# Routed experts computed only for the tokens that chose them, by scatter through device memory

## The reference, cut to what matters

```python
scores = sigmoid(x @ gate_w.T)                 # [2048, 16]
topk_w, topk_ids = top_k(scores, 4); topk_w /= topk_w.sum(-1)
comb[t, topk_ids[t]] = topk_w[t]               # zero for the other 12 experts
eo = (silu(x @ Wg[e]) * (x @ Wu[e])) @ Wd[e]   # for every e
out = (silu(x @ sg) * (x @ su)) @ sd + sum_e comb[:, e] * eo[e]
```

## Time and profile before

| | us |
|---|---|
| median of three runs | 1480.97 |
| profiled execution, own time | 1483.09 |
| its span (first to last instruction) | 1481.7 |
| first matmul of `experts(0)` (L923) | 1141.10 |
| last group of matmuls of `experts(1)` (L940) begins | 1475.68 |

### The profile page before, as it was taken

One profiled execution on the slowest core, in us unless ns is written; L12 is line 12 of the kernel. 1 busy time (PEld: TensorE's weight loads), 2 busy tenths in 40 slices (PEclk: granted clock), 3 DMA queues, 4 the chain that ended last, 5 costly groups with the idle time before them and its releaser, 6 DMA issues.

```text
span 1481.7 us, 19507 instructions
## 1 busy us (share of the span) xinstructions
PE 1232.3 (83%) x7048; PEld 748.6 (51%) x7048; DVE 889.1 (60%) x2091; ACT 599.9 (40%) x1205; POOL 327.0 (22%) x327
## 2 busy tenths in 40 slices
PE   4568868976479934699999899898978999999998
PEld 2234645653336621243335333265544778777777
DVE  3676638575938575767675776177787575542322
ACT  2232146322255621356554465644435343232222
POOL 3410023220443220600000200033321232222222
PEclk9789998985889975799999999999997999999999
DMA  6144530360024300133322020060000000000000
GB/s 180 64 90 93 79 49 1 72 87 1 0 75 86 44 0 0 61 68 44 44 44 44 1 44 2 1 182 1 0 1 1 1 1 15 1 15 1 15 1 15
DMA packets 45919, 56.44 MB, mean 38 GB/s; under 512 B 8742, under 2 KB 30592, under 8 KB 45824
## 3 DMA queue, kind: packets, MB, share of 16 engines
q1 hardware_dynamic: 45824, 55.20, 18.6%
HBM read 40.37 MB, written 14.68 MB: 37 GB/s over the span
## 4 chain that ended last, share of the span: by engine, by line
PE 62%; DVE 22%; ACT 7%; issue 5%; POOL 2%; DMA 2%; SPq 0%; DVEq 0%; ACTq 0%; POOLq 0%
PE psum L923 12%; PE psum L940 7%; PE psum L814 5%; PE psum L602 5%; PE psum L784 4%; PE psum L833 4%; PE psum L684 3%; DVE mx L1639 3%; PE psum L709 2%; PE psum L695 2%; PE psum L503 2%; DVE stats L1254 2%; DVE small L1419 1%; PE psum L584 1%; PE psum L927 1%
## 5 line engine op out<-in xcount | busy, mean ns | idle before, releaser
L1639 DVE TENSOR_REDUCE mx<-psum 128x1 f32<-128x512 f32 (+3 forms) x384 | 200.1, 552 | 87.4 <-PE psum L787 63.1
L1865 POOL TENSOR_TENSOR work<-work,small 128x308 f32<-128x308 f32 x128 | 90.9, 713 | 312.6 <-DVE small L1435 312.6
L923 PE MATMUL psum<-H_r,area_r 128*128 128x512 f32 x408 | 145.6, 398 | 0.0
L1927 POOL TENSOR_TENSOR work_r<-work,work_r 128x512 fp32r<-128x512 f32 x68 | 89.3, 1313 | 250.1 <-ACT work_r L1214 250.1
L784 PE MATMUL psum<-stack_area 96*128 96x512 bf16 (+3 forms) x288 | 100.3, 353 | 45.9 <-DVE mx L1639 44.5
L1766 DVE TENSOR_TENSOR work<-work,psum 128x512 f32<-128x512 f32 x68 | 46.7, 687 | 150.3 <-PE psum L923 148.2
L1155 ACT ACTIVATE work<-psum 128x512 f32<-128x512 f32 (+1 forms) x192 | 94.7, 526 | 78.5 <-PE psum L836 59.9
L684 PE MATMUL psum<-area 128*128 128x308 f32 x256 | 100.7, 479 | 20.1 <-DVE work L1432 15.8
L1214 ACT CAST work_r<-work 128x512 fp32r<-128x512 f32 x68 | 42.2, 620 | 164.3 <-DVE work L1770 157.9
L1155 ACT ACTIVATE HT<-psum 128x384 f32<-128x384 f32 (+2 forms) x192 | 82.4, 454 | 47.6 <-PE psum L836 31.5
L833 PE MATMUL psum<-stack_area 98*128 98x512 bf16 (+3 forms) x288 | 94.9, 336 | 7.1 <-ACT work L1155 3.6
(11 more groups left out here) (254 smaller groups left out, 2721.5 us busy)
## 6 DMA issues: line engine op xcount, KB each, us to landing
stack_area<-parts_a0q SPq DMA_DIRECT2D x24, 128.0 KB, 4.2
stack_area<-parts_a0k SPq DMA_DIRECT2D x24, 128.0 KB, 7.0
stack_area<-parts_a1q SPq DMA_DIRECT2D x24, 128.0 KB, 4.6
stack_area<-parts_a1k SPq DMA_DIRECT2D x24, 128.0 KB, 7.2
stack_area<-parts_d0q SPq DMA_DIRECT2D x18, 128.0 KB, 4.3
stack_area<-parts_d0k SPq DMA_DIRECT2D x18, 128.0 KB, 7.1
stack_area<-parts_d1q SPq DMA_DIRECT2D x18, 128.0 KB, 4.1
stack_area<-parts_d1k SPq DMA_DIRECT2D x18, 128.0 KB, 6.7
```

The lines of the kernel that those rows point to most:

```text
L923: done = pe.matmul(u.bank(x), w[:, c, :], h[:, c, cols], start=k == 0, stop=k == len(products) - 1)
L1639: dve.tensor_reduce(mx[:, j, t, half:half + 1], u.bank(k)[:, 0:cols], AX.X, ALU.max).then_inc(*u.empties(k))
L1865: pool.tensor_tensor(ex3, ex3, small[:, of_i + 4:of_i + 8].unsqueeze(2).to_broadcast([P, HPG, CTX]), ALU.mult).then_inc(ctx_prob, 1)
L1927: pool.tensor_tensor(work_r[x % 4][:, :], work[x % 4][:, :], work_r[4 + x % 4][:, :], ALU.subtract).then_inc(act_lo, 1)
```

## The change: what it does

The 16 routed experts are applied to the rows that chose them. The tokens of a batch, four rows each, are sorted by expert through a tensor in device memory of 48 tiles of 128 rows; each expert's part begins at a tile, so 32 full tiles and the parts that are not full fit in 48, and all 48 are always computed. A row has 272 words: 256 values, and 16 words (one for each expert) that say where its result goes. What a tile does not fill is set beforehand to rows whose results go nowhere (1e6 is out of bounds for the scatter).

- `between("contexts")` on GpSimd makes a 128 x 272 tile of unused rows; `between("softmax")` on ScalarE writes it over both tensors with eight DMAs (6144 x 272 words each tensor, 13.4 MB in all), ahead of the L1224 casts.
- `route(b)`: no three-part split, no token split, no weight split. TensorE counts (one matmul, 7 and 8 narrower bf16 ones) how many earlier rows chose each expert; VectorE works out weight, slot, tile's expert and offset of each row and tile (some 20 operations of 16 to 768 elements); GpSimd issues 32 indirect DMAs (8 tiles x 4 choices), each scattering 128 rows of 1088 bytes.
- `experts(b)`: 28 units of two tiles, 4 of the shared expert (tokens as they lie in HT) and 24 routed, in 31 steps. Step n handles four units at once: gate and up of unit n-1, turn of hidden n-2, down of n-3, turn of the rows of n. TensorE reads the expert's offset from memory into a register (`value_load`) before each tile's matmuls, 4 times a routed unit. ScalarE copies the turned rows (512 columns), takes Silu (256), copies the result (512); VectorE multiplies, copies hidden, and works out where rows go; GpSimd scatters the unit's results by two indirect DMAs of 128 rows of 1 KB; SyncE loads a unit's rows (278 KB) three units ahead, the first after all 32 scatters have landed.
- `combine(b)`: for each of 8 tiles SyncE loads four results a token (512 KB, two buffers), VectorE multiplies each by its weight and adds it to X (four operations that wait for each other). The output is stored by half a batch afterwards.
- The order: `route(1)` and `context_out(1,"e")` go two steps to each step of `experts(0)`; `combine(0)` goes beside `experts(1)` from its step 8; `combine(1)` runs alone at the end.

```diff
-            weave(e["context"](1, "e"), chain(e["context_out"](0, "e"), e["route"](0), e["split_first"]()))
-            weave(e["experts"](0), chain(e["context_out"](1, "e"), e["route"](1)))
-            drain(e["experts"](1))
+            weave(e["context"](1, "e"), chain(e["context_out"](0, "e"), e["route"](0)))
+            advance(e["experts"](0), other := chain(e["context_out"](1, "e"), e["route"](1)), extra_every=1)
+            drain(other)
+            advance(e["experts"](1), other := e["combine"](0), COMBINE_START)
+            drain(other)
+            drain(e["combine"](1))
 # tensor_engine, route(b); pauses of ROUTE_STEPS = 11 and TILES * TOPK = 32 steps
+                pe.wait_ge(chosen_done, b + 1)
+                pe.matmul(bank[:, 0:P], earlier_bf, m.chosen.rearrange("p t e -> p (t e)"), start=True, stop=False, skip_group_check=True)
+                for t in range(TILES - 1):
+                    ...
 # tensor_engine, experts(b)
+                for n in range(UNITS + UNIT_STEPS):
+                    x, g, h, d = n, n - 1, n - 2, n - 3
+                    if 0 <= g < UNITS:
+                        routed = g - SHARED_UNITS
+                        if routed >= 0:
+                            pe.wait_ge(*u_x.empty(routed))
+                        ...
+                        for q in range(UNIT_TILES):
+                            at = pe.value_load(m.offset[0:1, ...], min_val=0, max_val=(EXPERTS - 1) * D) if routed >= 0 else 0
+                            for c in range(DC):
+                                if routed >= 0:
+                                    lhs, w = rows_t[routed % 2][:, q, c, :], wgu[c][:, bass.ds(at, D)]
+                                ...
+                                done = pe.matmul(u_g.bank(g)[:, q * D:(q + 1) * D], lhs, w, ...)
+                    if 0 <= h < UNITS:
+                        ...  # two transposes of hidden
+                    if 0 <= d < UNITS:
+                        ...  # for each tile value_load and one matmul, 256 columns of wd
+                    if SHARED_UNITS <= x < UNITS:
+                        pe.wait_ge(unit_landed[slot].sem, 16 * use)
+                        ...  # four transposes of the unit's rows
+                    yield
 # scalar_engine, between("softmax"), ahead of the L1224 casts
+                    act.wait_ge(unused_set, 2)
+                    for b in range(BATCH):
+                        for part in range(4):
+                            slots = slice(part * SLOTS // 4, (part + 1) * SLOTS // 4)
+                            act.dma_start(rows_dram[b][slots, :].rearrange("(s p) n -> p s n", p=P),
+                                          unused_rows[:, :].unsqueeze(1).to_broadcast([P, SLOTS // 4 // P, ROW])).then_inc(*unused_stored.up())
 # scalar_engine, experts(b), one step
+                    if 0 <= g < UNITS:
+                        act.activation(hidden[g % 2], u_g.bank(g)...[:, :, 0:INNER], ACT.Silu).then_inc(silu_done, 1)
+                    if SHARED_UNITS <= d < UNITS:
+                        act.copy(unit_out[routed % OUT_SLOTS][:, :], u_d.bank(d)).then_inc(*u_d.empties(d))
+                    if SHARED_UNITS <= x < UNITS:
+                        act.copy(rows_t[routed % 2]..., u_x.bank(routed)).then_inc(*u_x.empties(routed))
 # gpsimd_engine, route(b)
+                pool.wait_ge(slots_done, b + 1)
+                for t in range(TILES):
+                    for k in range(TOPK):
+                        at = t * TOPK + k
+                        pool.indirect_dma_start(rows_dram[b], bass.IndirectOffsetOnAxis(m.slot_k[:, at:at + 1], 0), m.rows[:, t, :],
+                                                None).then_inc(*dispatched[b].up())
+                        yield
 # gpsimd_engine, experts(b), for d of a routed unit
+                        pool.wait_ge(*u_down[b].empty(d))
+                        for q in range(UNIT_TILES):
+                            pool.indirect_dma_start(outs_dram[b], bass.IndirectOffsetOnAxis(m.out_row[:, tile:tile + 1], 0),
+                                                    unit_out[routed % OUT_SLOTS][:, q * D:(q + 1) * D], None, bounds_check=SEQ * TOPK - 1,
+                                                    oob_is_err=False).then_inc(*out_landed[routed % OUT_SLOTS].up())
 # sync_engine, experts(b) and combine(b)
+                        if routed == 0:
+                            sp.wait_ge(dispatched[b].sem, 16 * TILES * TOPK)
+                        if routed >= ROW_SLOTS:
+                            sp.wait_ge(*u_rows[b].full(routed - ROW_SLOTS))
+                        ...
+                        sp.dma_start(unit_rows[slot], rows_dram[b][routed * UNIT_TILES * P:(routed + 1) * UNIT_TILES * P, :]
+                                     .rearrange("(s p) n -> p s n", p=P)).then_inc(*unit_landed[slot].up())
+                for t in range(TILES):
+                    if t >= 2:
+                        sp.wait_ge(x_final[b], t - 1)
+                    sp.dma_start(returned_rows[b][t % 2], by_token[t]).then_inc(*returned_landed[t % 2].up())
```

More of the change, by code:

```diff
@@ new lines, in build, with routing_memory, take @@
+        wgu_shared = [carve(area[c], 7888, D) for c in range(DC)]
+        wd = carve(stack_area, 4096, EXPERTS * D)
+        wd_shared = carve(area[0], 8144, D)
+        unused_rows = carve(area[1], 9216, ROW)
+        earlier_bf, ones_bf = [carve(area[0], at, P // 2, BF16) for at in (8400, 8464)]
+        class Routing:
+            pass
+        def routing_memory(b):
+            m, at = Routing(), [TILES * ROW]
+            def take(n, dt=F32):
+                at[0] += n
+                return carve(area[b], at[0] - n, n, dt)
+            m.rows = carve(area[b], 0, TILES * ROW).rearrange("p (t n) -> p t n", t=TILES)
+            m.sc, m.rank = [take(P).rearrange("p (t e) -> p t e", t=TILES) for _ in range(2)]
+            m.col = take(TILES)
+            m.chosen = take(P // 2, BF16).rearrange("p (t e) -> p t e", t=TILES)
+            m.slot = take(P).rearrange("p (t e) -> p t e", t=TILES)
+            m.comb_k = take(TILES * TOPK)
+            m.slot_k = take(TILES * TOPK, I32)
+            m.slot_f, m.row_f = take(TILES * TOPK), take(ROUTED_UNITS * UNIT_TILES)
+            m.tiles, m.first, m.end = [take(EXPERTS) for _ in range(3)]
+            m.expert = take(ROUTED_UNITS * UNIT_TILES)
+            m.offset = take(ROUTED_UNITS * UNIT_TILES, I32)
+            m.out_row = take(ROUTED_UNITS * UNIT_TILES, I32)
+            m.is_k = take(TILES * TOPK * EXPERTS).rearrange("p (t k e) -> p t k e", t=TILES, k=TOPK)
+            m.of_k = H[b][:, 4:6, :].rearrange("p a d -> p (a d)").rearrange("p (t k e) -> p t k e", t=TILES, k=TOPK)
+            m.wide = H[b][:, 0:3, :].rearrange("p a d -> p (a d)")
+            m.is_expert = carve(area[1], 8144 + b * 768, 768).rearrange("p (s e) -> p s e", e=EXPERTS)
+            return m
@@ new lines, in build @@
+        hidden = [work[2][:, n * D:(n + 1) * D].rearrange("p (s i) -> p s i", s=UNIT_TILES) for n in range(2)]
+        hidden_t = [work[3][:, n * D:(n + 1) * D].rearrange("p (s n) -> p s n", s=UNIT_TILES) for n in range(2)]
+        unit_out = [work[4 + n] for n in range(OUT_SLOTS)]
+        of_expert = [work[7][:, n * 2 * EXPERTS:(n + 1) * 2 * EXPERTS].rearrange("p (s e) -> p s e", s=UNIT_TILES) for n in range(2)]
+        returned_rows = [[H[b][:, n * TOPK:(n + 1) * TOPK, :] for n in range(2)] for b in range(BATCH)]
@@ new lines, in route @@
+                dve.wait_ge(*steps.now())
+                dve.tensor_reduce(m.tiles, by_tile, AX.X, ALU.add).then_inc(*steps.up())
+                dve.wait_ge(*steps.now())
+                dve.tensor_tensor(by_expert, before, m.tiles.unsqueeze(1).to_broadcast([P, EXPERTS, EXPERTS]), ALU.mult).then_inc(*steps.up())
+                dve.wait_ge(*steps.now())
+                dve.tensor_reduce(m.first, by_expert, AX.X, ALU.add).then_inc(*steps.up())
+                dve.wait_ge(*steps.now())
+                dve.tensor_tensor(m.end, m.first, m.tiles, ALU.add).then_inc(*steps.up())
@@ L1915, in route @@
                 yield from normalise(b, "f", None, None)
[L1916 to L1928 removed]
+                yield from pause(ROUTE_STEPS)
@@ new lines, in combine, with between @@
+            def combine(b):
+                yield from pause(TILES)
+            def between(where):
+                if where == "contexts":
+                    pool.wait_ge(*u_out["a", 1].full(7))
+                    pool.memset(unused_rows[:, 0:D], 0.0).then_inc(unused_set, 1)
+                    pool.memset(unused_rows[:, D:ROW], NOWHERE).then_inc(unused_set, 1)
+                elif where == "masked":
+                    for c in range(SPANS):
+                        pool.wait_ge(*u_heads["d"][BATCH - 1, GROUPS - 1, c].empty(1))
+                    pool.memset(ones_bf, 1.0).then_inc(ones_bf_set, 1)
@@ L1934, in gpsimd_engine @@
```

(4 more changed lines are left out.)

474 lines of the change are left out of this document (256 added, 218 removed).

## The result

| | before | changed |
|---|---|---|
| median, us | 1483.19 | 1552.03 |
| lowest to highest | 1480.32 to 1488.81 | 1549.26 to 1557.85 |
| profiled execution, own time | 1483.09 | 1549.26 |
| its span | 1481.7 | 1547.9 |

The changed kernel is slower: ratio 1.046, 95% interval 1.042 to 1.051. The forecast was 1500, so direction and range (1450 to 1590) held and the size didn't: 4.6% slower instead of 1.3%.

The account below looks back on a forecast made before the run. TensorE's throughput was taken to bound the experts, then a routed loop of 4.9 us steps. Stages ending at 1484.4 plus 16 for the fill gave a span of 1500.4, forecast median 1500 us against a span of 1481.7; range 1450 to 1590.

Parts of the forecast that it names:

- TensorE's part: Matmuls and transposes of one routed unit: 3.52 us; with shared units 192 us instead of 320, a gain of 128.
- The loop of a step: Routed step: ScalarE's copy of the rows before the next gate adds 0.66 us, giving 4.18 before register loads.
- Register loads: Four per routed unit on TensorE's sequencer: 0.7 us a step, between 0 and 1.7, making a step 4.9 us.
- Rival A: Faster: the sequencer hides the register loads in 48 routed steps, worth 34 us, giving 1466; chance 0.17.
- The scatter: Each indirect DMA holds GpSimd 1.3 us, between 0.25 and 2.2; sets when batch 0's first routed unit can start.
- rival B: Same: a scatter costs GpSimd 0.5 us or less, dispatch ends before TensorE arrives, saving 23 us, giving 1477; chance 0.12.
- `experts(1)`: Batch 1's expert stage: 133.1 us, to 1453.3, its rows waited for under the shared units.
- The fill: ScalarE stalls 31.5 us issuing eight DMAs, delaying the casts and spline copy: +16 us, between 0 and +58.
- The end: After the last matmul: scatters and landing 4.9, combine(1) alone 23.2, store 3.0 us; end at 1484.4.
- rival D: Slower: gaps drop TensorE's clock to 1.2 GHz half the time in 48 routed steps, 84 us, giving 1584; chance 0.12.
- Rival C: Slower: a scatter costs GpSimd 2.0 us, +22 in the first dispatch, +50 - 2 in experts(0), giving 1570; chance 0.13.
- E: Faster: the fill doesn't stall ScalarE because the queue is deep enough, giving 1484, the same; chance 0.08.

Follow-up runs that it names:

- e8: Changed kernel with fill spread and rows transposed behind gate and up, now without register loads (tile number modulo 16 replaces the offset); 1449.7 us, ratio 0.977.
- e2: Changed kernel without its 192 register loads, tile number modulo 16 taking the place of the loaded expert offset; 1500.4 us, ratio 1.011.
- e3: Changed kernel with the same four register loads a unit, all moved to the head of the step; 1517.7 us, ratio 1.023.
- e9: Changed kernel with fill spread and rows transposed behind gate and up, down reusing gate's registers (two loads a unit, not four); 1471.4 us, ratio 0.993.
- e1: Changed kernel with the eight fill DMAs spread, one at the head of each softmax group; 1531.9 us, ratio 1.032.
- e7: Changed kernel with four buffers instead of two for batch 1's returned rows; 1549.7 us, ratio 1.048.
- e5: Changed kernel with results leaving by SyncE's plain stores instead of GpSimd's scatter, not sent back to their tokens; 1539.7 us, ratio 1.038.
- e6: Changed kernel with six extra, unread identity transposes on TensorE in each routed step of batch 1; 1557.8 us, ratio 1.052.
- the control: The changed kernel itself, unaltered, run again in a later set on another chip; 1546.8 us, ratio 1.043.
- c1: Changed kernel with fill spread, loads at step head, rows behind gate and up, four buffers; first run 1493.1 us (1.007), second 1473.5 us (0.994).
- c5: Changed kernel with fill spread, rows behind gate and up, two loads, four buffers, batch 1's context_out, normalising and rankings early; 1494.3 us, ratio 1.008.

## Why the size was wrong

**TensorE's part** (3.52 us a unit, forecast): 3.25 in e8. Right, the saving is there.

**The loop of a step** (4.18 without loads): 4.24 in e2. Right.

**Register loads** (0.7 a step, bounds 0 and 1.7): 1.3. This is the step that failed. "The two that stand first behind a wait cannot be hidden, the other two can" was wrong twice. A load takes the sequencer 0.7 us and not 0.35, and the exposed ones are others: gate's first behind the copy (idle 1.46 with it, 0.73 without), and down's second, between two pairs (down 1.41 to 1.46 instead of 1.03), while down's first is over before its matmuls are due. 48 steps x 0.6 us = 29 of the 36.9 us missed in the experts. With the 5.9 of `experts(1)` below and 4.8 of slow gates in batch 1 (from its first routed gate to its last 131.8 us, against 127.0 for 23 steps of 5.52, the mean of those without a slow gate) that is 40, so some 3 came back. In batch 0 the same stretch takes 142.4 us, 15 more than those 127 with slow gates and all, where I had 17 for route(1) and GpSimd alone. Rival A, loads hidden, is refuted, and e3 and e9 show that moving or halving them only helps as far as queued matmuls cover them.

**The scatter** (1.3 us): 0.96 and 0.30 between two, 1.27. Right, and so were the end of dispatch(0) (1196.6 against 1193.4 with the fill) and the first routed matmul (1201.0 against 1199). The Trainium skill, "DMA: Bandwidth & Descriptors", section "Anatomy of one DMA — SWDGE (gpsimd) path", has descriptor generation small beside the receipt; here a scatter of 128 rows lands after 2.4 us and holds GpSimd for 1.27 of them, so the rule's rival B falls.

**`experts(1)`** was to have its rows under the shared units. It waited 5.9 us, because GpSimd took the scatters of dispatch(1) between results until 1366.

**The fill** (+16): +20.2, shown by e1. The spline's copy came as forecast: ScalarE issued for 34.45 us where I had 31.5, but from 499.3 instead of 501.5, and the copy came at 544.5 instead of 543.8. The other 4 us came behind it (17.8 late at ScalarE's next table load, 554.07 against 536.26; 20.2 at the weights' loads, 987.52 against 967.28), and what costs them isn't shown.

**The end** (31.1): 35.6. combine(1) took 26.2 from its first issue; e7 shows that 6.8 of that is waiting for a buffer.

**The clock** (rival D, 1584): windows of 20 us alternate between 1.00 and 0.91, and in the 0.91 ones a gate takes 3.3 to 3.8 us. The Trainium skill, "TensorE: Matmul & The Clock Gate", section "A second HAM failure mode: psum-queue depth-cycling", says that gaps between groups make the clock swing. The trace agrees in that the clock swings in a kernel with such gaps; e5 and e6 leave open whether the gaps do it. Its worth is 4.8 us in batch 1 of this trace and half of that in the control's, where the rival had 84 for both batches. Rival C (scatter 2.0) and E (the fill doesn't stall) are refuted by the rows above.

**Two sums of the prediction** were off by little: 83 us of scatters against 78 is 5 and not 2, and A with a third of B and E is 0.24 and not 0.26.

## What to carry to other kernels

When work is cut below a throughput bound, write down the loop that is left, engine by engine, and ask for each wait in it what could be issued before it: moving four transposes ahead of independent work gave 54 us, as much as leaving out all 192 register loads (52). A value that the tensor engine's sequencer must load from memory cost 0.7 us here unless matmuls already queued covered it; put it where the queue is full, and read the price from a kernel without it. Bulk DMAs of many small pieces go one at a time between other work, not in a row on an engine that has something to do.

## What the runs showed of the hardware, unexpected

- A register load takes TensorE's sequencer 0.7 us: TENSOR_LOAD 0.30, FUSED_REGOPS 0.15 and SEQ_ASSERT 0.02, with gaps between them. From the end of ScalarE's copy to the gate behind it are 0.78 us with a load between (changed kernel and e9) and 0.06 without (e2); four in a row followed each other at 0.7.
- Eight DMAs of 1536 pieces each held ScalarE 34.45 us at their issue; one at a time they cost it nothing that shows.
- On two of the five chips (the second and the last set) ScalarE's silu of a shared unit stood 26.0 to 27.7 us while GpSimd scattered the rows of batch 0, though TensorE had long delivered. In the first run of c1:
```profile
1183.61 0.66 ACT L1251 ACTIVATE work<-psum 128x256 f32<-128x256 f32 x2 [27.73 <-remote]
```
  The wait is put down to `remote`, and ScalarE has such waits in all six traces of these chips and in none of the others. In c1 they come again among the routed steps, up to 7.86 us, and three routed gates have 5.06 to 8.63 us of idling ahead of them. Its first routed gate is 9 us later than in the second run (1191.3 against 1182.2) and batch 1's first is 22 later (1369.6 against 1347.4), so the 20 us went there. It is not the landing of the first unit's rows: in c5 ScalarE went on at 1166.73, before SyncE issued that load (1171.40). The cause isn't known; it was not tried by itself.
